# Zero rows below the operands of a few tensor products

## The chip, the cores and the metric

One NeuronCore of a Trainium2 chip runs the whole program in one launch. The metric is the device time in microseconds (us) of an execution. The kernel before takes 1612.25 us, the median of three runs (1609.80 to 1613.06 us).

TensorE (PE) multiplies, ScalarE (ACT) and VectorE (DVE) do the element-wise work and read the matmul results, GpSimd (POOL) prepares constants and a few small steps, SyncE (SP) issues most DMAs. Each engine works through its own list in order and waits at semaphores for the others.

## The reference

The input x has 32 batches of 128 tokens with 128 features, and a context of the same shape. Four layers follow, each an attention on the context and then a feed-forward part; each part adds `tanh(gate) * part(layernorm(x))` to x. What matters here are the biases and one selection:

```python
# layer 0, attention: the output product has a bias bo
out = out @ Wo + bo
# layer 0, feed-forward: a short convolution along the tokens with a bias conv_b per feature
# layer 1, feed-forward: 3-tap convolution over 512 hidden features, with bias
h = depthwise_conv1d(h.transpose(0, 2, 1), conv_w, conv_b)
# layer 2, attention
pv = jnp.einsum('nle,fe->nlf', v, Wv) + bv
# layer 2, feed-forward: one of 8 experts for each token, by the argmax of a softmax
probs = jax.nn.softmax(x @ Wg + bg, axis=-1)
e_idx = jnp.argmax(probs, axis=-1) % 8
h = jax.nn.relu(jnp.einsum('bsd,edf->besf', x, We) + be[None, :, None, :])
out = jnp.einsum('besf,bse->bsf', h, onehot) * p[..., None]
```

## The kernel before, in words

The program runs eight stages one after the other: A0, F0, A1, F1, A2, F2, A3, F3 (A is attention, F is feed-forward, the digit is the layer). Each stage goes over eight chunks of four batches (CB = 4, 512 tokens). x stays in SBUF. A stage starts a chunk when the stage before has finished that chunk of x (semaphore `x_done`). Inside a stage the order of each engine's instructions is written out by hand in Python functions, with a loop over pairs of chunks; PE issues the first products of chunk c + 1 between the last ones of chunk c.

A matmul takes a stationary operand (loaded by a LDWEIGHTS instruction, which the profile lists as the engine PEld) and a moving operand; both lie on partitions, and the number of partitions is the number of rows that are summed over. An f32 product is two passes, so two LDWEIGHTS and two MATMUL records.

A bias is added by a product of its own that opens the accumulation in PSUM: a stationary operand of ones times the bias. In before.py these products have few rows:

- L936, stage A0, one per chunk: `ones[0:1, :]` times one row of `bo0`, f32, 1 row, ahead of the output products L938.
- L1102, stage F0, `conv`, one per chunk: `ones[0:1, :]` times `cb0`, f32, 1 row, ahead of the 16 convolution products L1105.
- L1269, stage F1, `up(c, p, j)`, four per chunk: `ones3` times `cbias1`, bf16, 3 rows. The three rows are the three bf16 parts into which the f32 bias is split (`parts`), so that the sum is exact. The three f32 tap products L1271 follow. Around them `integers_T` (L1279, transposes of the quantised hidden values) and `down` (L1288) of three steps earlier are issued. `down` waits for ACT's copy of those transposes (L1460) and, at the first step of a chunk, for DVE's update of x (L2408).
- L1168, stage A2, `projected`, one per chunk: `ones3` times `biasv2`, bf16, 3 rows, ahead of the value products L1170.
- L1325, stage F2, `logits`, one per chunk: `ones3` times `bias2`, bf16, 3 rows, ahead of L1327.
- L1339, stage F2, `spread(c, e)`, eight per chunk: `select2[:, e, :]` times `ohT2[0:E2, :]`, bf16, 8 rows. It copies row e of the transposed one-hot choice onto all 128 partitions; DVE multiplies the tokens by it (L2490, `masked`), and the expert product L1347 uses the masked tokens. `spread` runs four experts ahead.
- L1343, stage F2, `bias`, one per chunk: `bepart2[0]` times `ohT2`, bf16, 24 rows (8 experts, three parts each).

In F2 `chosen` (L1334) transposes the one-hot choice `oh2` that DVE makes at L2483, ACT copies it to `ohT2` (L1821), and the first `spread` of the next chunk waits for that copy. DVE's order in a chunk is: masked 0 to 3, residual, masked 4, masked 5, the argmax with L2474 to L2483, masked 6 and 7, normalisation.

POOL prepares the constants: those of A1, A2, F1 and F0 after its last share of A0, those of F2 after its last share of F1; after each it waits for DVE's variance (`power`, L602).

Of the kernel before, what the change touches and what calls it, by code (L numbers as in the profile page):

```python
# [6 lines left out]
BF16 = mybir.dt.bfloat16  # L7
# [53 lines left out]
RING2 = 4  # L61
# [76 lines left out]
def flamingo(nc, a, out):  # L138
    ctx = ExitStack()
    with ctx:  # L140
        def sb(name, shape, dt=F32):
            return ctx.enter_context(nc.sbuf_tensor(name, shape, dt))
# [26 lines left out]
        ident16 = sb("ident16", [P, P], BF16)  # L169
        ones = sb("ones", [P, P])  # L170
# [32 lines left out]
        def ar(shape, dt=F32):  # L203
            n = 1
            for s in shape[1:]:
                n *= s
            words = n if dt != BF16 else (n + 1) // 2
            v = arena[0:shape[0], used[0]:used[0] + words]
            used[0] += words
            assert used[0] <= ARENA  # L210
            v = v if dt == F32 else v.bitcast(dt)
            if len(shape) == 3:
                v = v.rearrange("p (a b) -> p a b", a=shape[1])
            if len(shape) == 4:
                v = v.rearrange("p (a b c) -> p a b c", a=shape[1], b=shape[2])
            return v
# [5 lines left out]
        lastdi3 = sb("last_places", [P, SC], U32)  # L222
        wq0, wkv0 = sb("wq0", [P, P]), sb("wkv0", [P, 2, 4 * D0])
        wkvs0 = sb("wkvs0", [P, KV0])
        wo0, bo0 = sb("wo0", [P, P]), sb("bo0", [P, P])
        bq0row, bq0 = sb("bq0row", [P, P]), sb("bq0", [P, CB * HEADS, D0])
        bk0g, bv0g, bkv0 = sb("bk0g", [P, 4 * D0]), sb("bv0g", [P, 4 * D0]), sb("bkv0", [P, KV0])
        wr0, rb0 = sb("wr0", [P, R0]), sb("rb0", [P, R0])
        wg0, wu0 = sb("wg0", [P, E0 * I0]), sb("wu0", [P, E0 * I0])
        wd0 = sb("wd0", [P, 2, P])  # L230
        cw0, cb0 = sb("cw0", [P, TAPS0]), sb("cb0", [1, P])
        wT1 = sb("wT1", [P, 3, P])
        causal = sb("causal", [P, P])
        w1q, w2q = sb("w1q", [P, H1], BF16), sb("w2q", [P, K1, P], BF16)
# [35 lines left out]
        wconv1 = ar([P, 3, H1])  # L270
        cb1, cbrest1 = ar([3, H1]), ar([3, H1])
        cbpart1 = [ar([3, H1], BF16) for _ in range(3)]
        cbias1, ones3 = ar([3, H1], BF16), ar([3, P], BF16)
        be2, berest2, bemask2 = ar([3 * E2, P]), ar([3 * E2, P]), ar([3 * E2, 3])
        bepart2 = [ar([3 * E2, P], BF16) for _ in range(3)]
        bg2, bgrest2 = ar([3, P]), ar([3, P])
        bgpart2 = [ar([3, P], BF16) for _ in range(3)]
        bias2 = ar([3, CB, P], BF16)
        select2 = ar([E2, E2, P], BF16)
        causal16 = ar([P, CB, P], BF16)  # L280
        bv2, bvrest2 = ar([3, P]), ar([3, P])
        bvpart2 = [ar([3, P], BF16) for _ in range(3)]
        biasv2 = ar([3, CB, P], BF16)

        fresh()
        wide0 = ar([P, CB, E0, I0])
# [31 lines left out]
        top2, nmx2, idx2, idf2 = ar([P, CB, 8]), ar([P, CB]), ar([P, CB, 8], U32), ar([P, CB])  # L318
        ex2, ps2, pg2 = ar([P, CB, P]), ar([P, CB]), ar([P, 2, CB])
        oh2 = ar([P, CB, 3 * E2])  # L320
        ohT2 = ar([3 * E2, W], BF16)
        xnT2 = [xnT, ar([P, W])]
        xm2 = ar([P, RING2, W])
        yT2 = ar([P, W])
# [85 lines left out]
        def context(p):  # L410
# [7 lines left out]
        ]  # L418
        SETUP_LOADS = [
            (graw[:, 0:4], rows(a["g_xattn"])), (graw[:, 4:8], rows(a["g_ffn"])), (graw[:, 8:9], rows(a["L3_xattn_gate"])),  # L420
            (bo0[:, :], rows(a["L0_xattn_bo"])),
            (wr0[:, :], a["L0_ffn_Wr"]), (rb0[:, :], rows(a["L0_ffn_router_bias"])),
            (wg0[:, :].rearrange("p (e i) -> p e i", e=E0), a["L0_ffn_Wg"].rearrange("e h i -> h e i")),
            (wu0[:, :].rearrange("p (e i) -> p e i", e=E0), a["L0_ffn_Wu"].rearrange("e h i -> h e i")),
# [12 lines left out]
            (wo3[:, :, :], a["L3_xattn_w_out"].rearrange("(k p) d -> p k d", p=P)), (bo3[:, :], rows(a["L3_xattn_b_out"])),  # L437
            (keyT[:, 0, :], a["L3_ffn_keys"]), (keyT[:, 1, :], a["L3_ffn_rw"]), (rb3[:, :], rows(a["L3_ffn_rb"])),
            (b13[:, :, :], a["L3_ffn_b1"].rearrange("e (k p) -> p e k", p=P)),
        ]  # L440

        WD = []
# [5 lines left out]
        s_const = sem("constants_ready")  # L448
# [31 lines left out]
        def _(sp):  # L480
            with nc.allow_non_contiguous_dma(reason="small vectors laid along the partitions"):
                sp.dma_start(FIRST_LOADS[0][0], FIRST_LOADS[0][1]).then_inc(s_first, 16)
                sp.dma_start(context(0), cview[:, 0:CB, :]).then_inc(s_cx[0], 16)
                for dst, src in FIRST_LOADS[1:]:
                    sp.dma_start(dst, src).then_inc(s_first, 16)
                sp.dma_start(context(1), cview[:, CB:2 * CB, :]).then_inc(s_cx[1], 16)
                sp.dma_start(wo0[:, :], a["L0_xattn_Wo"]).then_inc(sem("wo0_loaded"), 16)
                sp.dma_start(x[:, 2 * CB:B, :], a["x"][2 * CB:B].rearrange("b t d -> t b d")).then_inc(sem("x_loaded"), 16)
                for dst, src in SETUP_LOADS:
                    sp.dma_start(dst, src).then_inc(s_load, 16)  # L490
            for dst, src in WD:
                sp.dma_start(dst, src).then_inc(s_wd, 16)

# [80 lines left out]
        def _(pl):  # L574
# [85 lines left out]
            def thrice(of):  # L660
                return of[:, :].unsqueeze(1).to_broadcast([3, CB, P])
# [1 line left out]
            pl.wait_ge(s_load, 16 * n_loads)  # L663
            pl.tensor_copy(causal16[:, :, :], causal[:, :].unsqueeze(1).to_broadcast([P, CB, P])).then_inc(sem("A12_constants"), 1)
            parts(bv2, bvrest2, bvpart2, lambda i: ident[0:3, i:i + 1])
            pl.tensor_tensor(biasv2[:, :, :], thrice(bvpart2[0]), thrice(bvpart2[2]), ALU.add).then_inc(sem("A12_constants"), 1)
            rest = cb1
            for i in range(3):
                step(pl.tensor_copy(cbpart1[i][:, :], rest[:, :]))
# [2 lines left out]
                rest = cbrest1  # L672
            for i in range(3):
                step(pl.tensor_scalar(cbpart1[i][:, :], cbpart1[i][:, :], ident[0:3, i:i + 1], None, ALU.mult))
            step(pl.tensor_tensor(cbias1[:, :], cbpart1[0][:, :], cbpart1[1][:, :], ALU.add))
            pl.tensor_tensor(cbias1[:, :], cbias1[:, :], cbpart1[2][:, :], ALU.add).then_inc(sem("F1_constants"), 1)
            pl.memset(ones3[:, :], 1.0).then_inc(sem("F1_constants"), 1)
            pl.wait_ge(s_setup, WEIGHTS)
            for t in range(3):
# [38 lines left out]
            step(pl.affine_select(out=bemask2[:, :], in_=bemask2[:, :], compare_op=ALU.is_ge, fill=0.0, base=E2 - 1,  # L718
                                  pattern=[[E2, 3]], channel_multiplier=-1))
            parts(be2, berest2, bepart2, lambda i: bemask2[:, i:i + 1])  # L720
            pl.tensor_tensor(bepart2[0][:, :], bepart2[0][:, :], bepart2[2][:, :], ALU.add).then_inc(sem("F2_constants"), 1)
            parts(bg2, bgrest2, bgpart2, lambda i: ident[0:3, i:i + 1])
            pl.tensor_tensor(bias2[:, :, :], thrice(bgpart2[0]), thrice(bgpart2[2]), ALU.add).then_inc(sem("F2_constants"), 1)
            pl.tensor_copy(select2[:, :, :], ident16[0:E2, 0:E2].unsqueeze(2).to_broadcast([E2, E2, P])).then_inc(sem("F2_constants"), 1)
            with pl.Fori(0, NC) as c:
                power("A2", c)
            with pl.Fori(0, NC) as c:
# [77 lines left out]
        def _(pe):  # L805
# [41 lines left out]
            def heads0():  # L847
# [35 lines left out]
                def body(c, p, more, first=False, live=True):  # L883


                    for w in range(STEPS0 if live else DRAIN0):
# [43 lines left out]
                        if tile:  # L930
                            cc, _, j = tile
                            if j == 0:
                                if first:
                                    pe.wait_ge(s_load, 16 * n_loads)
                                pe.wait_ge(s_xdone, cc + 1)
                                nc.tensor.matmul(bank[7][:, :], ones[0:1, :], bo0[0:1, :].unsqueeze(1).to_broadcast([1, CB, P]), start=True, stop=False)  # L936
                            pe.wait_ge(sem("A0_oT"), cc * CB + (j + 3))
                            nc.tensor.matmul(bank[7][:, j * P:j * P + P], oT0[:, j % 2, :], wo0[:, :], start=False, stop=(j == CB - 1))\  # L938
                                .then_inc(sem("A0_y"), 1)
# [158 lines left out]
            def conv(c):  # L1098

                pe.wait_ge(sem("F0_conv_in"), c + 1)  # L1100
                pe.wait_ge(s_xdone, c + (NC * STAGE["F0"] + 1))
                nc.tensor.matmul(bank[5][:, :], ones[0:1, :], cb0[:, :].unsqueeze(1).to_broadcast([1, CB, P]), start=True, stop=False)  # L1102
                for j in range(CB):
                    for k in range(TAPS0):
                        nc.tensor.matmul(bank[5][:, j * P:j * P + P], cin0[:, j, k:k + P], taps0[:, k, :], start=False, stop=False)  # L1105
# [230 lines left out]

            def spread(c, e):
                pe.wait_ge(sem("F2_masked"), c * E2 + (e + 1))
                nc.tensor.matmul(bank[2 + e % RING2][:, :], select2[:, e, :], ohT2[0:E2, :], start=True, stop=True).then_inc(sem("F2_spread"), 1)  # L1339

            def bias(c):
                pe.wait_ge(sem("F2_relu"), c + 1)
                nc.tensor.matmul(bank[6][:, :], bepart2[0][:, :], ohT2[:, :], start=True, stop=False).then_inc(sem("F2_bias"), 1)  # L1343

            def expert(c, e):
                pe.wait_ge(sem("F2_masked"), c * E2 + (e + 1 + RING2))
# [112 lines left out]
        def _(act):  # L1459
# [1201 lines left out]
```

## Time and profile before

| what | value |
|---|---|
| median of three runs | 1612.25 us (1609.80 to 1613.06) |
| profiled execution, its own time | 1613.21 us |
| its span, first to last instruction | 1611.4 us |
| PE busy | 1416.8 us, 88% |
| PE weight loads | 1027.8 us, 64% |
| DVE busy | 1106.9 us, 69% |
| ACT busy | 1023.7 us, 64% |
| POOL busy | 543.4 us, 34% |
| share of PE in the chain that ended last | 68% |
| mean granted TensorE clock | 0.957 |

Busy time is a union of the instructions' durations; since matmuls are pipelined, the duration of one (for example 0.38 us) is longer than the distance from its start to the next one's start (for example 0.22 us). The distance between starts is what a stream of matmuls costs. A clock of 1.00 is the upper of TensorE's two levels (2.4 GHz), 0.50 the lower (1.2 GHz).

### The profile page before, as it was taken

How to read it: one execution, taken by the hardware profiler on the slowest of the kernel's cores; microseconds unless marked ns; L12 is line 12 of the kernel's file. 1: busy time of each engine (PE TensorE's matmuls, PEld its weight loads, DVE VectorE, ACT ScalarE, POOL GpSimd, SP SyncE). 2: the span in 40 equal slices, each digit the busy share in tenths (PEclk: the TensorE clock that was granted, in tenths of full speed). 3: DMA queues.
4: the chain of work that ended last, by engine and by line, in shares of the span. 5: the costliest groups of instructions: out<-in, count | busy, mean ns of one | idle time of the engine just before them, and what ended most of it. 6: DMA issues, size and time to landing. Idle time of an engine off the chain costs nothing.

```text
span 1611.4 us, 35134 instructions
## 1 busy us (share of the span) xinstructions
PE 1416.8 (88%) x9978; PEld 1027.8 (64%) x9982; DVE 1106.9 (69%) x3551; ACT 1023.7 (64%) x2947; POOL 543.4 (34%) x627
## 2 busy tenths in 40 slices
PE   2788888998989989899999989999997389999994
PEld 2566655666734446343466666666666289999994
DVE  1788887688767656787467767777777546666665
ACT  2688887554545556222778868788875367777762
POOL 5354466222211221001001413422433635555550
PEclk9899999999989999899999999999997589999998
DMA  8000049700299931000000100100032322222227
GB/s 193 24 8 7 13 69 164 103 0 7 60 165 164 166 49 38 1 1 0 8 8 2 35 19 18 35 22 13 28 125 89 103 60 66 63 67 66 67 58 261
DMA packets 143559, 98.41 MB, mean 61 GB/s; under 512 B 20610, under 2 KB 132652, under 8 KB 142292
## 3 DMA queue, kind: packets, MB, share of 16 engines
q1 hardware_dynamic: 134740, 80.15, 26.1%
q0 software_dynamic: 8704, 16.87, 3.2%
q8 instruction: 55, 0.90, 0.2%
q14 instruction: 60, 0.49, 0.1%
HBM read 43.10 MB, written 54.93 MB: 61 GB/s over the span
## 4 chain that ended last, share of the span: by engine, by line
PE 68%; ACT 11%; DVE 10%; issue 7%; POOL 2%; DMA 1%; SPq 0%; DVEq 0%; ACTq 0%; POOLq 0%
PE bank L983 7%; PE bank L1427 7%; PE bank L1419 7%; PE bank L1271 5%; PE bank L999 4%; PE bank L1034 4%; PE bank L1347 4%; PE bank L924 4%; ACT arena L1460 3%; PE bank L1019 3%; ACT att L1597 3%; PE bank L987 3%; PE bank L1009 3%; ACT att L1462 2%; PE bank L906 2%
## 5 line engine op out<-in xcount | busy, mean ns | idle before, releaser
L1460 ACT ACTIVATE arena<-bank 128x512 f32<-128x512 f32 (+7 forms) x396 | 254.9, 672 | 155.6 <-PE bank L1334 57.9
L1881 ACT ACTIVATE att<-bank,arena 128x128 f32<-128x128 f32 x576 | 165.0, 371 | 73.2 <-PE bank L1419 73.0
L800 POOL DMA_INDIRECT expert_outputs<-arena x144 | 143.6, 997 | 146.6 <-DVE arena L2601 133.2
L1597 ACT ACTIVATE att<-bank,arena 128x128 f32<-128x128 f32 x512 | 180.7, 396 | 15.7 <-DVE arena L2119 14.7
L754 POOL DMA_INDIRECT dispatched_rows<-arena x112 | 115.4, 1030 | 172.0 <-DVE arena L2027 84.6
L602 POOL TENSOR_TENSOR ve<-mv,eps 128x4 f32<-128x4 f32 x64 | 12.9, 202 | 462.8 <-DVE mv L1943 454.9
L1427 PE MATMUL bank<-arena,att 128*128 128x128 f32 x1152 | 153.9, 277 | 1.0 <-ACT att L1881 0.3
L1419 PE MATMUL bank<-xnT,arena 128*128 128x128 f32 x1152 | 154.0, 277 | 0.2 <-ACT xnT L1460 0.2
L1427 PEld LDWEIGHTS bank<-arena,att 128*128 128x128 f32 x1152 | 140.9, 193 | 3.1 <-ACT att L1881 3.1
L1419 PEld LDWEIGHTS bank<-xnT,arena 128*128 128x128 f32 x1152 | 141.6, 194 | 0.6 <-ACT xnT L1460 0.6
L1597 ACT ACTIVATION_READ_ACCUMULATOR att<-bank,arena 128x1 f32 x512 | 120.9, 236 | 0.0
L2587 DVE COPY arena<-arena 128x512 f32 x144 | 61.6, 427 | 83.0 <-issue 82.9
L1460 ACT ACTIVATE xnT<-bank 128x128 f32<-128x128 f32 (+1 forms) x180 | 63.6, 354 | 85.3 <-PE bank L821 35.6
L2119 DVE TENSOR_REDUCE arena<-bank 128x4 f32<-128x512 f32 x128 | 82.4, 685 | 49.6 <-PE bank L999 49.4
L1582 ACT ACTIVATE arena<-bank 128x512 f32<-128x512 f32 x128 | 76.1, 615 | 58.1 <-PE bank L983 58.1
L2042 DVE TENSOR_REDUCE nmx<-bank 128x8 f32<-128x1024 f32 x64 | 78.0, 1219 | 44.4 <-PE bank L895 43.9
L924 PE MATMUL bank<-ident,att 128*128 128x128 f32 x512 | 69.6, 279 | 28.7 <-ACT att L1462 28.3
L1271 PE MATMUL bank<-arena 128*128 128x512 f32 x192 | 92.5, 618 | 0.0
L2125 DVE TENSOR_TENSOR att<-att,arena 128x512 f32<-128x512 f32 x128 | 89.2, 696 | 4.9 <-DVE arena L2124 0.5
L999 PE MATMUL bank<-arena 64*128 64x128 f32 x1024 | 78.2, 293 | 13.2 <-ACTq L1589 6.6
L999 PEld LDWEIGHTS bank<-arena 64*128 64x128 f32 x1024 | 65.5, 195 | 34.5 <-issue 27.1
L924 PEld LDWEIGHTS bank<-ident,att 128*128 128x128 f32 x512 | 55.9, 142 | 45.6 <-ACT att L1462 45.3
(360 smaller groups left out, 3255.1 us busy)
## 6 DMA issues: line engine op xcount, KB each, us to landing
dispatched_rows<-padf SPq DMA_DIRECT2D x16, 2128.5 KB, 34.7
arena<-dispatched_rows SPq DMA_DIRECT2D x144, 64.5 KB
cxT<-in_ctx SPq DMA_DIRECT2D x32, 256.0 KB, 2.8
arena<-in_L_ffn_w SPq DMA_DIRECT2D x8, 1024.0 KB
arena<-expert_outputs SPq DMA_DIRECT2D x8, 1024.0 KB, 13.9
expert_outputs<-arena POOLq DMA_INDIRECT x144
out_x<-x SPq DMA_DIRECT2D x8, 256.0 KB, 4.3
dispatched_rows<-arena POOLq DMA_INDIRECT x112
```

Source lines behind the costliest of these rows:

```text
L754: pl.indirect_dma_start(sent, bass.IndirectOffsetOnAxis(places[:, q:q + 1], 0), held[:, q, :], None)\
L800: pl.indirect_dma_start(sent_out, bass.IndirectOffsetOnAxis(xtu3[:, s, P:P + 1], 0), yt3[:, s, :], None, bounds_check=TOP3 * TOKENS - 1, o ...
L924: last = nc.tensor.transpose(bank[2 + k][:, i * P:i * P + P], ex[:, v % 2 * 2 + k, i, :], ident[:, :])
L983: last = nc.tensor.matmul(A[:, :], wqk3[:, t, pair * P:pair * P + P], cxT[:, p, :] if t else xnT[:, :], start=True, stop=True)
L999: last = nc.tensor.matmul(bank[side][:, i * P:i * P + P], q, k, start=True, stop=True)
L1271: last = nc.tensor.matmul(bank[1 + j][:, :], xsT1[:, p * CB + j, t:t + P], wconv1[:, t, :], start=False, stop=(t == 2))
L1419: last = nc.tensor.matmul(bank[s % 2][:, k * P:k * P + P], w1c3[:, s % 4, k * P:k * P + P], xnT[:, (s % 4) * P:(s % 4) * P + P], start=Tru ...
L1427: last = nc.tensor.matmul(bank[2 + s % 2][:, 0:P], h3[:, s % 2, k * P:k * P + P], w2c3[:, s % 4, k * P:k * P + P], start=(k == 0), stop=(k ...
L1460: copy = lambda o, i: nc.scalar.activation(o, i, ACT.Copy)
L1597: last = nc.scalar.activation(ex3_of(w, side)[:, i, :], bank[side][:, i * P:i * P + P], ACT.Exp, bias=nm3[:, w % 2, h:h + 1], accum_out=su ...
L1881: last = nc.scalar.activation(h3[:, s % 2, k * P:k * P + P], bank[s % 2][:, k * P:k * P + P], ACT.Gelu, bias=b1c3[:, s % 4, k:k + 1])
L2125: v.tensor_tensor(ex3_of(w, side), ex3_of(w, side), rs3[:, w % 2, side:2 * HQ:2].unsqueeze(2).to_broadcast([P, HQ, P]), ALU.mult) .then_in ...
```

## The change

The few-row operands become operands of 128 rows, in which all rows behind the old ones are zero (in `ones` and `ones3` they are ones, against zero rows of the other operand). Names: `bo0` becomes `boz0`, loaded as one row into a zeroed tile by the last setup load, which waits for POOL's constants; `cb0` is copied into the zeroed `cbz0`; `cbias1`, `ones3`, `bias2`, `biasv2`, `select2` and `ohT2` get 128 partitions; `be16` is new and takes the sum of `bepart2`. `ohT2` moves to the arena's part for constants, where it is zeroed once; ACT's copy still writes its first 24 rows. POOL gets nine memsets and one copy. Number, order and columns of all matmuls stay as they are.

```diff
-        cbias1, ones3 = ar([3, H1], BF16), ar([3, P], BF16)
+        cbias1, ones3 = ar([P, H1], BF16), ar([P, P], BF16)
-        bias2 = ar([3, CB, P], BF16)
-        select2 = ar([E2, E2, P], BF16)
+        bias2 = ar([P, CB, P], BF16)
+        select2 = ar([P, E2, P], BF16)
+        be16 = ar([P, P], BF16)
+        ohT2 = ar([P, W], BF16)
-        biasv2 = ar([3, CB, P], BF16)
+        biasv2 = ar([P, CB, P], BF16)
...
-            (bo0[:, :], rows(a["L0_xattn_bo"])),
+            (boz0[0:1, :], a["L0_xattn_bo"].rearrange("(a d) -> a d", a=1)),
...
-                for dst, src in SETUP_LOADS:
+                for dst, src in SETUP_LOADS[:-1]:
                     sp.dma_start(dst, src).then_inc(s_load, 16)
+                sp.wait_ge(s_const, 1)
+                sp.dma_start(SETUP_LOADS[-1][0], SETUP_LOADS[-1][1]).then_inc(s_load, 16)
...
+            pl.memset(boz0[:, :], 0.0)
...
+            step(pl.memset(biasv2[:, :, :], 0.0))
+            pl.tensor_tensor(biasv2[0:3, :, :], thrice(bvpart2[0]), thrice(bvpart2[2]), ALU.add).then_inc(sem("A12_constants"), 1)
+            step(pl.memset(cbias1[:, :], 0.0))
+            pl.memset(ohT2[:, :], 0.0)
...
+            step(pl.memset(cbz0[:, :], 0.0))
+            pl.tensor_copy(cbz0[0:1, :], cb0[:, :])
...
+            step(pl.memset(be16[:, :], 0.0))
+            step(pl.memset(bias2[:, :, :], 0.0))
+            step(pl.memset(select2[:, :, :], 0.0))
...
-                                nc.tensor.matmul(bank[7][:, :], ones[0:1, :], bo0[0:1, :].unsqueeze(1).to_broadcast([1, CB, P]), start=True, stop=False)
+                                nc.tensor.matmul(bank[7][:, :], ones[:, :], boz0[:, :].unsqueeze(1).to_broadcast([P, CB, P]), start=True, stop=False)
...
-                nc.tensor.matmul(bank[5][:, :], ones[0:1, :], cb0[:, :].unsqueeze(1).to_broadcast([1, CB, P]), start=True, stop=False)
+                nc.tensor.matmul(bank[5][:, :], ones[:, :], cbz0[:, :].unsqueeze(1).to_broadcast([P, CB, P]), start=True, stop=False)
...
-                nc.tensor.matmul(bank[2 + e % RING2][:, :], select2[:, e, :], ohT2[0:E2, :], start=True, stop=True).then_inc(sem("F2_spread"), 1)
+                nc.tensor.matmul(bank[2 + e % RING2][:, :], select2[:, e, :], ohT2[:, :], start=True, stop=True).then_inc(sem("F2_spread"), 1)
...
-                nc.tensor.matmul(bank[6][:, :], bepart2[0][:, :], ohT2[:, :], start=True, stop=False).then_inc(sem("F2_bias"), 1)
+                nc.tensor.matmul(bank[6][:, :], be16[:, :], ohT2[:, :], start=True, stop=False).then_inc(sem("F2_bias"), 1)
```

## Rows read from the trace of the kernel before

**Rows 1.** Busy time by stretch: length, busy of each engine, clock, DMA share, GB/s.

```profile
451.00:579.00 128.00, 120.19 (x490) 56.18 (x490) 87.48 (x342) 70.68 (x129) 28.41 (x48) 0.98 1.19 156
641.00:756.00 115.00, 109.76 (x372) 46.20 (x371) 92.45 (x349) 25.17 (x88) 10.87 (x18) 0.93 0.00 1
```

**Rows 2.** Few-row products by line: count, ns min/median/max, first and last start us, shape.

```profile
L1269 PE MATMUL bank<-arena x32: 382/385/604, 453.2 to 575.0; 3*128 3x512 bf16 x32
L1339 PE MATMUL bank<-arena x64: 374/384/629, 651.8 to 751.8; 8*128 8x512 bf16 x64
```

**Rows 3.** Timeline of PE in F2: start us, us from first start to last end.

```profile
671.78 0.38 PE L1339 MATMUL bank<-arena 8*128 8x512 bf16 x1
672.00 0.38 PE L1325 MATMUL bank<-arena 3*128 3x512 bf16 x1
672.31 1.16 PE L1327 MATMUL bank<-wg,xnT 128*128 128x128 f32 x8
...
675.95 1.98 PE L1347 MATMUL bank<-arena,we 128*128 128x512 f32 x4
677.77 0.60 PE L1334 MATMUL bank<-ident,arena 128*24 128x128 f32 x4
678.21 1.88 PE L1347 MATMUL bank<-arena,we 128*128 128x512 f32 x4
680.02 0.39 PE L1339 MATMUL bank<-arena 8*128 8x512 bf16 x1
```

**Rows 4.** The same timeline in A1, around a 128-row bf16 product.

```profile
430.67 0.39 PE L1186 MATMUL bank<-arena,ident 128*128 128x512 bf16 x1
430.89 1.05 PE L1190 MATMUL bank<-arena 128*128 128x128 f32 x8
```

**Rows 5.** Timeline of all engines in F1; in brackets idle before, and releaser.

```profile
507.13 0.58 ACT L1460 ACTIVATE arena<-bank 128x512 bf16<-128x512 bf16 x1
507.77 0.40 PE L1288 MATMUL bank<-w2q,arena 128*128 128x128 bf16 x4
508.32 0.38 PE L1269 MATMUL bank<-arena 3*128 3x512 bf16 x1
508.63 0.30 PEld L1271 LDWEIGHTS bank<-arena 128*128 128x128 f32 x2 [0.23 <-issue]
508.63 2.84 PE L1271 MATMUL bank<-arena 128*128 128x512 f32 x6
511.51 0.60 ACT L1790 ACTIVATE arena<-bank 128x512 f32<-128x512 f32 x1 [1.79 <-PE bank L1271]
...
516.37 0.34 PE L1288 MATMUL bank<-w2q,arena 128*128 128x128 bf16 x3 [0.92 <-DVE x L2408]
```

**Rows 6.** Timeline of DVE: the one-hot choice in F2.

```profile
676.76 0.26 DVE L2483 TENSOR_TENSOR arena<-iota,arena 128x96 f32<-128x96 f32 x1
```

**Rows 7.** Timeline of DVE in A2.

```profile
622.69 1.13 DVE L2334 SCALAR_TENSOR_TENSOR x<-bank,rsg,x 128x128 f32 x4 [0.31 <-PE bank L1208]
```

**Rows 8.** Timeline in A0, behind the bias product.

```profile
133.51 1.12 PE L936 MATMUL bank<-bo,ones 1*128 1x512 f32 x2
134.57 0.49 PE L938 MATMUL bank<-wo,arena 128*128 128x128 f32 x2
134.93 1.05 ACT L1462 ACTIVATE att<-att 128x1024 f32<-128x1024 f32 x1
136.11 1.09 PE L924 MATMUL bank<-ident,att 128*128 128x128 f32 x8
```

**Rows 9.** Who waited for whom in F0: us in total, times, longest us.

```profile
PE bank L1113 <- ACT arena L1460: 5.8, 7, 1.1
```

**Rows 10.** Timeline of POOL: a memset, and its first wait behind the constants of F2.

```profile
4.03 0.54 POOL L609 MEMSET arena<- 64x512 bf16 x1
574.39 0.28 POOL L602 TENSOR_TENSOR ve<-mv,eps 128x4 f32<-128x4 f32 x1 [5.16 <-DVE mv L1943]
```

**Rows 11.** Busy time in a stretch of A3, columns as in rows 1.

```profile
954.00:963.00 9.00, 6.94 (x47) 6.44 (x47) 1.29 (x2) 3.69 (x17) 3.83 (x4) 0.62 0.14 42
```

More of the change, by code:

```diff
@@ L224, in flamingo @@
         wkvs0 = sb("wkvs0", [P, KV0])
-        wo0, bo0 = sb("wo0", [P, P]), sb("bo0", [P, P])
+        wo0 = sb("wo0", [P, P])
         bq0row, bq0 = sb("bq0row", [P, P]), sb("bq0", [P, CB * HEADS, D0])
@@ L231, in flamingo @@
         cw0, cb0 = sb("cw0", [P, TAPS0]), sb("cb0", [1, P])
+        cbz0 = sb("cbz0", [P, P])
+        boz0 = sb("boz0", [P, P])
         wT1 = sb("wT1", [P, 3, P])
@@ L320, in flamingo @@
         oh2 = ar([P, CB, 3 * E2])
-        ohT2 = ar([3 * E2, W], BF16)
         xnT2 = [xnT, ar([P, W])]
@@ L665, in _ @@
             parts(bv2, bvrest2, bvpart2, lambda i: ident[0:3, i:i + 1])
-            pl.tensor_tensor(biasv2[:, :, :], thrice(bvpart2[0]), thrice(bvpart2[2]), ALU.add).then_inc(sem("A12_constants"), 1)
+            step(pl.memset(biasv2[:, :, :], 0.0))
+            pl.tensor_tensor(biasv2[0:3, :, :], thrice(bvpart2[0]), thrice(bvpart2[2]), ALU.add).then_inc(sem("A12_constants"), 1)
+            step(pl.memset(cbias1[:, :], 0.0))
+            pl.memset(ohT2[:, :], 0.0)
             rest = cb1
@@ L674, in _ @@
                 step(pl.tensor_scalar(cbpart1[i][:, :], cbpart1[i][:, :], ident[0:3, i:i + 1], None, ALU.mult))
-            step(pl.tensor_tensor(cbias1[:, :], cbpart1[0][:, :], cbpart1[1][:, :], ALU.add))
-            pl.tensor_tensor(cbias1[:, :], cbias1[:, :], cbpart1[2][:, :], ALU.add).then_inc(sem("F1_constants"), 1)
+            step(pl.tensor_tensor(cbias1[0:3, :], cbpart1[0][:, :], cbpart1[1][:, :], ALU.add))
+            pl.tensor_tensor(cbias1[0:3, :], cbias1[0:3, :], cbpart1[2][:, :], ALU.add).then_inc(sem("F1_constants"), 1)
             pl.memset(ones3[:, :], 1.0).then_inc(sem("F1_constants"), 1)
@@ L720, in _ @@
             parts(be2, berest2, bepart2, lambda i: bemask2[:, i:i + 1])
-            pl.tensor_tensor(bepart2[0][:, :], bepart2[0][:, :], bepart2[2][:, :], ALU.add).then_inc(sem("F2_constants"), 1)
+            step(pl.memset(be16[:, :], 0.0))
+            step(pl.memset(bias2[:, :, :], 0.0))
+            step(pl.memset(select2[:, :, :], 0.0))
+            pl.tensor_tensor(be16[0:3 * E2, :], bepart2[0][:, :], bepart2[2][:, :], ALU.add).then_inc(sem("F2_constants"), 1)
             parts(bg2, bgrest2, bgpart2, lambda i: ident[0:3, i:i + 1])
-            pl.tensor_tensor(bias2[:, :, :], thrice(bgpart2[0]), thrice(bgpart2[2]), ALU.add).then_inc(sem("F2_constants"), 1)
-            pl.tensor_copy(select2[:, :, :], ident16[0:E2, 0:E2].unsqueeze(2).to_broadcast([E2, E2, P])).then_inc(sem("F2_constants"), 1)
+            pl.tensor_tensor(bias2[0:3, :, :], thrice(bgpart2[0]), thrice(bgpart2[2]), ALU.add).then_inc(sem("F2_constants"), 1)
+            pl.tensor_copy(select2[0:E2, :, :], ident16[0:E2, 0:E2].unsqueeze(2).to_broadcast([E2, E2, P])).then_inc(sem("F2_constants"), 1)
             with pl.Fori(0, NC) as c:
@@ L1820, in chosen_T @@
                     act.wait_ge(sem("F2_bias"), c)
-                copy(ohT2[:, :], bank[0][0:3 * E2, :]).then_inc(sem("F2_ohT"), 1)
+                copy(ohT2[0:3 * E2, :], bank[0][0:3 * E2, :]).then_inc(sem("F2_ohT"), 1)
             def exponentials(c):
```

## Prediction

> **What bounds the kernel now.** Begin with the page: the chain that ended last is PE for 68% of the span. A change to PE's stream can therefore count, if it lies in stages that PE bounds. The busy time by stretch says which: in F1 PE is busy 120.2 of 128 us, in F2 109.8 of 115, both near the full clock (0.98 and 0.93) [rows 1]. The lines with few rows come next: L1269 has 32 records in F1, L1339 has 64 in F2 [rows 2]; by the loops, L1168, L1325 and L1343 have 8 each, and L936 and L1102 have 8 products of two passes each. The durations in that view say nothing, since matmuls overlap. The timeline of PE does, read by distances between starts.
>
> Take F2 [rows 3]. From L1334 at 677.77 to L1347 at 678.21 four transposes cost 0.44, 0.11 each. A 512-column f32 pass, of which L1347 has four between 678.21 and 680.02, costs 1.81/4; in the clean stretches elsewhere it is 0.43, so 1.72 for the four, and 0.09 is left over, just ahead of the 8-row L1339. The four passes that follow an L1339 (675.95 to 677.77) take 1.82: 0.10 too much, this time just behind it. And the L1339 at 671.78 costs 0.22 when the 3-row L1325 follows at 672.00, but that one costs 0.31 when the 128-row L1327 follows. So a few-row product is itself no slower than its 512 columns (0.22). What costs is each change between few rows and 128 rows: about 0.10 going in, 0.10 coming out, and 0.10 more behind the first 128-row pass (half of that behind a bf16 or identity transpose). The weight loads show why: the two LDWEIGHTS of L1271 begin only at 508.63, together with its first matmul, after 0.23 of idle [rows 5]; they weren't loaded ahead. The counter-example is in A1: L1186 is bf16, 512 columns, 128 rows, and the f32 product behind it starts 0.22 later, at 430.89 [rows 4]. No stall on a product that is the same but for its rows.
>
> **The change, part by part.** It leaves every product in its place with 128 rows in both operands, so the changes of rows go.
>
> *Price of one.* An isolated one, such as L1269, saves 0.10 + 0.10 + 0.10 = 0.30 on PE (508.32 to 508.63 is 0.31 where rows 4 have 0.22, and so on) [rows 4, 5]. A group of four L1339 ahead of transposes saves 0.10 + 0.09 + 0.05 = 0.24, once. The 1-row f32 product L936 takes 133.51 to 134.57, 1.06 where two passes are 0.86; with 0.09 ahead and 0.10 behind that is 0.39 [rows 8].
>
> The Trainium skill weighs in on both sides. "TensorEngine Tiling (Array Packing)", Key Properties, has it that changing the tiling mode drains TensorE, which would be this stall, and the trace agrees. "TensorE: Matmul & The Clock Gate", in the table "Why this matters for your kernels", says that a single matmul with K = 32 takes the same time as one with K = 128; by that alone widening would give nothing, which is rival A.
>
> *F2.* One chunk of PE holds a group of four (0.24), L1343 (0.30), L1339 ahead of a transpose (0.25), L1339 with L1325 (0.30) and two isolated L1339 ahead of L1347 (0.30 each): 1.68 of the 12.93 between 667.09 and 680.02. But PE isn't alone there. L1334 transposes what DVE makes at L2483, which ends at 677.02, and L1334 starts at 677.77 [rows 3, 6]: 0.75 later. All the savings of the chunk lie ahead of L1334, while DVE's order up to L2483 is one unbroken run that starts with the first L1339; after 0.75 PE waits for it. The same pair stands 1.13, 0.75, 0.56, 0.35, 0.56, 0.56 and 1.13 apart in the seven chunks that have it, 5.03 in sum. To each, 0.09 is added (no stall ahead of the next chunk's L1339, behind L1334) and a wake-up of 0.05 taken off: 5.3. The last chunk has no such pair but three masked products of DVE at its end: 0.25. The L1325 before the first chunk: 0.25. F2 gives 5.8, of at most 8 x 1.68 = 13.4.
>
> *F1.* Four L1269 a chunk, 0.30 each. Two are covered. Behind the second one, PE's L1288 waits for ACT's copy (507.13 + 0.58 = 507.71, L1288 at 507.77) [rows 5]; ACT is busy without a break from the silu of the first one, so that one gains nothing. The last of a chunk runs beside the DVE run that begins with the silu of the third (ACT L1790 at 511.51) and ends with x, for which PE has idled 0.92 before 516.37; its gain becomes idle time. Two count: 0.60 in each of five middle chunks, 3.0. The first chunk has no ACT wait behind the second product, but a half-clock start: 1.0. In the seventh DVE does less and three count, 0.9. In the last all four, less the one behind a wait: 1.1. F1 gives 6.0, of at most 32 x 0.30 = 9.5.
>
> *A2.* PE runs back to back; the period could fall by 0.30. The next in line is DVE's loop, which idles 0.31 for PE at L2334 [rows 7]: just enough. One of eight products lies in the end of F1, where PE waits anyway; six at 0.28 and the half-clock one at 0.3 give 2.0, of at most 2.4.
>
> *A0.* 0.39 a chunk on PE, and the products behind L936 would come earlier, but L924 at 136.11 waits for ACT's exponential, which ends at 134.93 + 1.05 = 135.98 [rows 8]. In all eight chunks the next L924 hangs on ACT or on the setup. I take 0, the other end is 8 x 0.39 = 3.1.
>
> *F0.* Behind L1102 and L1105, PE waits for ACT before L1113 in seven chunks, 5.8 in all [rows 9], 0.8 each. So 0.39 counts in the first chunk alone: 0.4, at most 3.1.
>
> *POOL.* A 512-element bf16 memset over 64 partitions took 0.54 [rows 10]; nine memsets and a copy are an estimated 5 us. The tightest place is ahead of 574.39, where POOL waits 5.16 behind the constants of F2 [rows 10]: 128 + 512 + 1024 elements, 1.8 by that row. Even at twice that it is hidden. The memsets of A1, F1 and F0 have 8.6 of waiting behind them, boz0 comes while the first loads are in flight. Without cover F2's would cost 1.8.
>
> *SP.* The last setup load now waits for POOL's constants, done at about 4 us, while SP issues it at about 33; the weight loads behind it on the queue don't wait either. A 64 KB broadcast becomes 0.5 KB. Nothing.
>
> Sum: 5.8 + 6.0 + 2.0 + 0 + 0.4 = 14.2 us. The profiled execution took 1613.2 (span 1611.4 and 1.8 around it), so 1599.0 for it; against the median of 1612.25, **1598 us**.
>
> **The rivals.**
>
> A. *Row count is not the cause.* The stall could come from the arena's few-row source tiles, or from the wait ahead of the product; then the 128-row ones stall as well and the time is 1612. For it: most few-row products stand behind a semaphore wait. Against: L1186 has such a wait in front too and doesn't stall, and L1325 behind L1339 is free [rows 3, 4].
>
> B. *More reaches the end than I let through.* If the waits for ACT and DVE move up with PE (because I took for an unbroken run what itself hangs on PE), the sum goes to PE's full 1.68 in F2 and 0.30 in F1: 13.4 + 9.5 + 2.4 + 0.4 = 25.7 us, and 1586.5. For it: PE idles so little in both [rows 1]. Against: the gaps of 0.75 and of 0.92 [rows 3, 5, 6].
>
> C. *The clock of A3 turns it slower.* The stretch 954 to 963 in A3 ran at a mean of 0.62: PE had idled there (6.94 busy in 9) [rows 11]. A mean of 0.62 over 9 us is 3.4 us of full-rate time lost, 6.8 us spent at the lower level, so a fall costs up to 3.4. All of A3 now begins 14 us earlier against whatever the clock goes by; if the falls came in five more of its chunks than before, 5 x 3.4 = 17 us would outweigh the 14.2, and 1615 would stand. It decides from five falls on. Against: PE idles no longer than before there, and only two chunks of A3's main part fall now. One fall more or less is quite possible and is in my range.
>
> **How the numbers follow.** My forecast has 0.73, A 0.07, B 0.15, C 0.05. A change under 0.2% (3.2 us) can't be told from none here. Faster by more: forecast and B, 0.88; within: A, 0.07; slower: C, 0.05. The range: the cover of each term is read to about 30% (4 us), a clock fall is 3.4 us either way, and the three runs shown spread 3 us. That gives 1592 to 1605 for the forecast alone; to leave no more than 2 in 10 out it reaches some way to B: 1589 to 1605.
>
> **What would show it.** Right: L1271's weight loads start ahead of its first matmul; L1269 costs 0.22 to the next start; the period in F2 falls from 12.93 to about 12.2 with L1334 now waiting for DVE's L2483; in F1 PE's wait for L2408 grows from 0.92 to 1.2 and a chunk shortens by 0.6; A0 and F0 keep their lengths but for 0.4; A3 and F3 keep theirs. Wrong: a stall in front of a 128-row L1339 (A), or an F2 period near 11.3 (B), or an unchanged start of A3. A wait of POOL under 1 us before A2's first variance would show the memsets dearer than taken.

## The result, and the profile after

The changed kernel took 1593.8 us (median of 6 runs, 1591.0 to 1595.8) beside 1611.0 for the kernel before (6 runs, 1608.5 to 1613.1): a ratio of 0.9895 [0.9881, 0.9909]. The same kernel once more (e10 below, on chip 15) gave 0.9896 [0.9879, 0.9912]. That is 17 us, where 14.2 were forecast; of the 4 us below the forecast of 1598, 1.2 are the kernel before itself, whose six runs have a median 1.2 lower than its first three. The chain of waits has less PE in it (61% for 68%) and more of DVE (13% for 10%) and ACT (13% for 11%). From the page of after (span, busy times, with POOL's eight memsets and one copy more, 636 instructions for 627, and the chain by engine):

```profile
span 1593.0 us, 35147 instructions
PE 1386.4 (87%) x9982; PEld 1032.8 (65%) x9982; DVE 1106.8 (69%) x3551; ACT 1023.0 (64%) x2947; POOL 547.8 (34%) x636
PE 61%; ACT 13%; DVE 13%; issue 8%; POOL 2%; DMA 1%; DVEq 1%; SPq 0%; ACTq 0%; POOLq 0%
```

Every line of PE is 14 further down now: L1339 is L1353 (the spread), L1343 is L1357, L1325 is L1339, L1334 is L1348 (`chosen`), L1347 is L1361 (the expert's passes), L1269 and L1271 are L1283 and L1285, L1288 is L1302, L924 is L938; DVE's L2483 is L2497, L2490 is L2504; ACT's L1460 and L1462 are L1474 and L1476.

PE's timeline in F2, after. It answers to [rows 3]:

```profile
672.57 0.38 PE L1353 MATMUL bank<-arena 128*128 128x512 bf16 x1
672.78 1.88 PE L1361 MATMUL bank<-arena,we 128*128 128x512 f32 x4
675.48 0.61 PE L1348 MATMUL bank<-ident,arena 128*24 128x128 f32 x4 [0.82 <-DVE arena L2497]
676.15 1.98 PE L1361 MATMUL bank<-arena,we 128*128 128x512 f32 x4
677.97 1.03 PE L1353 MATMUL bank<-arena 128*128 128x512 bf16 x4
...
684.16 0.38 PE L1353 MATMUL bank<-arena 128*128 128x512 bf16 x1
684.38 1.02 PE L1361 MATMUL bank<-arena,we 128*128 128x512 f32 x2
```

L1353 costs 0.21 or 0.22 to the next start (672.57 to 672.78, 684.16 to 684.38), whatever stands on either side. And L1348 now waits 0.82 for DVE's one-hot, where before it came 0.75 behind it.

The timeline of F1, after, answers to [rows 5]. The weight loads of L1285 begin at 497.46, 0.22 ahead of its first pass and beside the bias product. L1302's wait for x is 1.29, from 0.99 for the same chunk of before (the next chunk, the one shown in [rows 5], went from 0.92 to 1.22):

```profile
496.54 0.40 PE L1302 MATMUL bank<-w2q,arena 128*128 128x128 bf16 x4 [1.29 <-DVE x L2422]
...
497.46 0.38 PE L1283 MATMUL bank<-arena 128*128 128x512 bf16 x1
497.46 0.41 PEld L1285 LDWEIGHTS bank<-arena 128*128 128x128 f32 x2
...
497.68 1.02 PE L1285 MATMUL bank<-arena 128*128 128x512 f32 x2
```

A0 shows a stall that goes and is given back at once, PE's timeline against [rows 8]. L950 costs 0.86 (131.88 to 132.74) where L936 cost 1.06. The next L938 (L924 in before, where it had no idle time ahead of it, 136.11 in [rows 8]) waits 0.46 for ACT's exponential:

```profile
131.88 1.02 PE L950 MATMUL bank<-boz,ones 128*128 128x512 f32 x2
132.74 0.39 PE L952 MATMUL bank<-wo,arena 128*128 128x128 f32 x2
...
134.57 1.09 PE L938 MATMUL bank<-ident,att 128*128 128x128 f32 x8 [0.46 <-ACT att L1476]
```

Where the time went, by the starts of the same instructions on PE in four profiles. Each row is the time from the mark of the row above to its own mark (us; e1 is the changed kernel with the old rows and e10 the changed kernel once more, both below):

| up to | before | e1 | after | e10 | forecast saving |
|---|---|---|---|---|---|
| F0's first convolution, from the start | 295.75 | 295.57 | 293.79 | 293.54 | 0 |
| A1's first scores | 107.45 | 107.41 | 107.37 | 107.36 | 0.4 |
| A1's last scores | 37.78 | 37.78 | 37.80 | 37.80 | 0 |
| A2's last scores (F1, A2) | 193.27 | 193.35 | 184.93 | 185.22 | 6.0 + 2.0 |
| first `chosen` of F2 | 15.80 | 15.81 | 14.89 | 15.98 | 0.25 |
| second `chosen` | 14.79 | 14.81 | 11.85 | 12.47 | 1.2 |
| last `back` | 92.83 | 92.84 | 89.82 | 89.87 | 4.4 |
| first product of F3's tiles (A3) | 536.42 | 533.39 | 534.83 | 532.71 | 0 |
| end of span (F3) | 317.34 | 317.01 | 317.70 | 317.19 | 0 |

F1 and A2 gave what was forecast. F2's total is near it, but made up otherwise: 2.3 to 2.9 in its first chunk and 3.0 in the other seven. Some 2 us come from the stretch before F0, where nothing was forecast. The row of A3 differs by 3.0 us between before and e1, which have the same products throughout, and tells nothing by itself.

### The profile page after: what moved, and what is told of

Read it like the earlier page. It is cut to its first block, busy times and chain, and to the rows that moved or that the text cites. A ratio compares the mean times of both kernels' runs of the same rounds, so it can differ in the third digit from the quotient of the medians.

```text
span 1593.0 us, 35147 instructions
## 1 busy us (share of the span) xinstructions
PE 1386.4 (87%) x9982; PEld 1032.8 (65%) x9982; DVE 1106.8 (69%) x3551; ACT 1023.0 (64%) x2947; POOL 547.8 (34%) x636
## 4 chain that ended last, share of the span: by engine, by line
PE 61%; ACT 13%; DVE 13%; issue 8%; POOL 2%; DMA 1%; DVEq 1%; SPq 0%; ACTq 0%; POOLq 0%
PE bank L997 7%; PE bank L1441 7%; PE bank L1433 7%; PE bank L1013 4%; ACT arena L1474 4%; PE bank L1048 4%; PE bank L1285 3%; PE bank L938 3%; PE bank L1033 3%; ACT att L1611 3%; PE bank L1001 3%; PE bank L1023 3%; ACT att L1476 2%; PE bank L920 2%; PE bank L1361 2%
## 5 line engine op out<-in xcount | busy, mean ns | idle before, releaser
L1474 ACT ACTIVATE arena<-bank 128x512 f32<-128x512 f32 (+7 forms) x396 | 255.0, 672 | 149.6 <-PE bank L1348 54.5
L1474 ACT ACTIVATE xnT<-bank 128x128 f32<-128x128 f32 (+1 forms) x180 | 63.6, 353 | 80.1 <-PE bank L835 34.3
L938 PE MATMUL bank<-ident,att 128*128 128x128 f32 x512 | 70.0, 280 | 32.2 <-ACT att L1476 32.0
L1285 PE MATMUL bank<-arena 128*128 128x512 f32 x192 | 89.7, 604 | 0.0
L938 PEld LDWEIGHTS bank<-ident,att 128*128 128x128 f32 x512 | 56.3, 142 | 49.1 <-ACT att L1476 48.4
```

The costliest lines, as they stand in the source:

```text
L938: last = nc.tensor.transpose(bank[2 + k][:, i * P:i * P + P], ex[:, v % 2 * 2 + k, i, :], ident[:, :])
L1285: last = nc.tensor.matmul(bank[1 + j][:, :], xsT1[:, p * CB + j, t:t + P], wconv1[:, t, :], start=False, stop=(t == 2))
L1474: copy = lambda o, i: nc.scalar.activation(o, i, ACT.Copy)
```

## The experiments

**How many rows does it take?** Four kernels have all of the change's set-up (memsets, copy, moved load) and another number of rows in the seven products; e1 has the old ones (1, 3, 8, 24). The edit is shown for `spread`, the other six read the same number of rows:

```
-    matmul(bank[2 + e % RING2], select2[:, e, :], ohT2[:, :])
+e1  matmul(bank[2 + e % RING2], select2[0:8, e, :], ohT2[0:8, :])
+e2  matmul(bank[2 + e % RING2], select2[0:32, e, :], ohT2[0:32, :])
+e3  matmul(bank[2 + e % RING2], select2[0:64, e, :], ohT2[0:64, :])
+e4  matmul(bank[2 + e % RING2], select2[0:65, e, :], ohT2[0:65, :])
```

> All of the change's set-up (memsets, copy, moved load) stays, but the seven products read only their old 1, 3, 8 or 24 rows again. Theory (the gain is all in the products' rows): the time of the kernel before, ratio 1.000 within 0.002, and L1285 again 0.31 behind its bias product. Rival (moving the load and zeroing matter): 2 to 4 us below the kernel before.

> The seven products read 32 rows of the widened tiles. Theory (a change of TensorE's row tiling stalls, and 32 rows are the same tiling as 3 or 8): no gain, ratio 1.000 within 0.002. Rival (few active rows as such make it slow, or the old tiles in the arena do): a part of the gain, above 4 us, or all of it, 17.

> The same with 64 rows. Theory (row tiling): 64 rows are still another tiling than 128, so the stalls of 0.10 stay on both sides and the ratio is 1.000 within 0.002. Rival (cost falls with the rows): about half of the 17 us.

> The same with 65 rows, one more than e3. Theory (row tiling, more than 64 rows take the whole array): the full gain, ratio 0.9895 within 0.002, no stall at the bias products. Rival (only exactly 128 rows match the neighbours): no gain, 1.000.

Measured: e1 1.0002 [0.9992, 1.0012], e2 1.0003 [0.999, 1.0015], e3 0.9993 [0.998, 1.0006], e4 0.99 [0.9883, 0.9918]. The set-up costs nothing that can be measured. Everything hangs on the 65th row. PE's timeline in F2, first of e3, then of e4:

```profile
673.90 0.39 PE L1353 MATMUL bank<-arena 64*128 64x512 bf16 x1
674.21 1.12 PE L1361 MATMUL bank<-arena,we 128*128 128x512 f32 x2
675.27 0.39 PE L1353 MATMUL bank<-arena 64*128 64x512 bf16 x1
675.59 1.98 PE L1361 MATMUL bank<-arena,we 128*128 128x512 f32 x4
```

```profile
672.89 0.38 PE L1353 MATMUL bank<-arena 65*128 65x512 bf16 x1
673.11 1.02 PE L1361 MATMUL bank<-arena,we 128*128 128x512 f32 x2
673.97 0.38 PE L1353 MATMUL bank<-arena 65*128 65x512 bf16 x1
674.19 1.88 PE L1361 MATMUL bank<-arena,we 128*128 128x512 f32 x4
```

The same source, semaphores and neighbours; from one spread to the next it is 1.37 at 64 rows (673.90 to 675.27) and 1.08 at 65. The same pair stands 1.37 apart at 8 rows (before and e1) and at 32 (e2), and 1.08 at 128. So the stall is neither the arena's nor the wait's (rival A), and it isn't graded: 1.37 less 1.08 is the 0.30 of the prediction within 0.01. What TensorE does in the stall, no run shows. It has the shape of the drain on a change of tiling mode in the Trainium skill's "TensorEngine Tiling (Array Packing)", Key Properties; that page gives no time for it.

**Do the stages add up?** e5 has 128 rows in F2's products alone, e6 in all but F2's.

```
 e5  # A0, F0, A2, F1: rows as before; F2: 128
 e6  # A0, F0, A2, F1: 128; F2: select2[0:8], be16[0:24], bias2[0:3]
```

> Only F2's three products (L1339, L1343, L1325) read 128 rows, the other four read their old rows. Theory (stalls plus a cover by DVE, and in F2's first chunk a clock that rises earlier): 5.5 to 7 us below the kernel before, ratio 0.996. Rival (F2 yields PE's full 1.68 a chunk once A2 no longer feeds it late): 13 us, 0.992. Rival (terms of the stages aren't additive, all of the gain needs all stages): under 3 us.

> The reverse: A0, F0, F1 and A2 at 128 rows, F2 at the old rows. Theory (additive): F0 0.4, F1 5.2, A2 about 2 to 3, so 8 to 9 us below before, ratio 0.9948, and together with e5 the 15 to 17 us of the whole. Rival (not additive): the sum of both is off by more than 4 us.

Measured: e5 1621.11, 0.9958 [0.994, 0.9976]; e6 1621.10, 0.9956 [0.9941, 0.9971]; before 1628.03 on that chip. 6.9 us each, 13.9 together; the intervals (3 us either way) hold both this and the 17 of the whole. F2 and the rest have a share of about one half each (5.8 and 8.4 were forecast); e6 is 1 to 2 us short of what was expected of it, within its interval.

**Why did F2's first chunk give 2.3 to 2.9 us?** It runs at the lower level of the clock (0.50 in the rows) at first. In the changed kernel the clock rises sooner. e7 is the changed kernel with the first four spreads of that chunk (RING2 is 4) at 8 rows, e8 the old rows with these four at 128; e12 and e11 do the same with every product of that chunk, and with the logits' bias of chunks 0 and 1:

```
 e7   rows = 8 if c == 0 and e < RING2 else 128      # the spread alone
 e8   rows = 128 if c == 0 and e < RING2 else 8
 e12  rows = 8 (24, 3) if c == 0 else 128        # spread, bias, logits' bias
 e11  rows = 128 if c == 0 else 8 (24, 3)
```

> The changed kernel, with only the first four spread products of F2's chunk 0 at 8 rows. Theory C (few-row products hold the granted clock at its lower level longer): the clock rises 6.5 us behind the first spread instead of 3.0 to 4.2, and chunk 0 (first to second L1348) takes about 14 us instead of 11.9 to 12.4. Theory S (only stalls): the rise stays at 3.0 to 4.2, chunk 0 takes at most 0.3 more. In total 2 us or 0.3 us, both near the noise; the profile decides.

> Old rows everywhere, with only the first four spread products of F2's chunk 0 at 128 rows. Theory C: the clock rises 3 to 4 us behind the first spread instead of 6.5 to 7.1, and chunk 0 takes about 13 us instead of 14.8. Theory S: 14.5 to 14.8 and the rise stays late. Total within 0.2% of before in both.

> The set-up of the changed kernel and the old row counts everywhere but in the first chunk of F2, which has all its products at 128 rows (8 spreads, one output bias, the logits' bias of chunks 0 and 1). Theory S (stalls alone, at whatever clock stands): five or six changes of rows go, most of them at half clock, and the clock rises when it rises, 6.2 to 7.4 us behind the first spread as in the runs with few-row products there: the chunk takes 14.0 to 14.4 us from `chosen` to `chosen`, not 14.8. Theory C (in this chunk the few-row products also hold the clock down): the rise comes 3 to 4.2 us behind the first spread, as in all five profiles with the wide products, and the chunk takes 11.9 to 12.5. In time S says about 0.6 us below before, C about 2.7 (0.9983).

> The inverse: the changed kernel with the old row counts in all products of F2's first chunk. S: the rise at 3 to 4.2 us stays, the chunk takes 12.5 to 13. C: the rise comes at 6.2 to 7.4 us and the chunk takes 14.8 to 15.2; the time is about 2.7 us above the changed kernel's, a ratio of 0.9912 to before where that one had 0.9895.

Measured: e7 0.9916 [0.9883, 0.995], e8 1.0003 [0.9991, 1.0015], e11 0.9966 [0.9951, 0.9982], e12 0.9911 [0.9894, 0.9929]. Two stretches of 3 us from the chunk's first spread on (length; busy time of PE, PEld, DVE, ACT, POOL; granted clock; DMA share, GB/s), of before, after, e11 and e12:

```profile
651.76:654.76 3.00, 3.00 (x6) 1.06 (x7) 2.21 (x4) 1.32 (x8) 0.00 (x0) 0.50 0.02 5
654.76:657.76 3.00, 3.00 (x8) 1.32 (x7) 1.21 (x4) 0.06 (x1) 0.00 (x0) 0.50 0.00 0
```

```profile
640.49:643.49 3.00, 3.00 (x7) 1.29 (x8) 2.21 (x4) 1.32 (x8) 0.00 (x0) 0.50 0.00 0
643.49:646.49 3.00, 3.00 (x17) 1.87 (x16) 2.15 (x8) 0.60 (x1) 0.00 (x0) 0.99 0.00 0
```

```profile
650.09:653.09 3.00, 3.00 (x7) 1.29 (x8) 2.21 (x4) 1.31 (x8) 0.00 (x0) 0.50 0.00 0
653.09:656.09 3.00, 3.00 (x14) 1.51 (x13) 1.84 (x7) 0.60 (x1) 0.00 (x0) 0.87 0.00 0
```

```profile
641.64:644.64 3.00, 3.00 (x6) 1.06 (x7) 2.21 (x4) 1.32 (x8) 0.00 (x0) 0.50 0.00 0
644.64:647.64 3.00, 3.00 (x8) 1.31 (x7) 1.21 (x4) 0.06 (x1) 0.00 (x0) 0.50 0.00 0
```

In the second stretch the clock is back (0.99, 0.87) where the chunk has no few-row product and still 0.50 where it has. In all 14 profiles:

| first chunk of F2 | clock rises, us behind the first spread | `chosen` to `chosen` |
|---|---|---|
| all at 128 (65) rows: after, e4, e5, e9, e10, e11 | 3.1, 4.2, 3.1, 3.8, 3.9, 3.8 | 11.85, 12.41, 11.87, 12.42, 12.47, 12.23 |
| few rows: before, e1, e2, e3, e6, e12 | 6.6, 6.6, 6.7, 7.1, 7.4, 7.4 | 14.79, 14.81, 14.83, 15.06, 15.19, 15.21 |
| mixed: e7, e8 | 6.3, 6.2 | 13.51, 14.85 |

Six of six against none of eight, and by e11 and e12 it goes with this chunk's own products, not with what comes before or behind. Nor does it go with how long before the first spread the clock fell: in e11 it fell 3.0 us ahead of it and stayed at 0.50 for 6.8 us, in e12 2.8 ahead and stayed for 10.2. All six kernels of the first line have 6.8 there, all eight others 10.2 or, where it didn't rise in between, 17.1. In e11 and e12 theory C of their expectations stands and S falls: the stalls of that chunk alone would save an estimated 0.4 to 0.8 us by the expectation of e11, and the chunk gives 2.3 to 3.4. e8 went against its theory C, which wanted the rise at 3 to 4 and a chunk of 13: four wide spreads don't bring the rise forward. Four few-row ones are enough to undo the early rise (e7, 6.3). What in the stalls holds the clock down the rows don't tell: PE is shown as busy for 3.00 of 3.00 in all. The run times agree where they can: e12 lies 3.5 us above e10 (by medians, on the same chip at another time, where the kernel before had moved by 1.2; the ratios' intervals overlap). e11 gained 5.3 us, more than the 2.6 of its chunk; A3's beginning had no clock fall in e11's profile, while before has one of 6.8 us at 784.6, which may be the rest. Falls there lasted 6.8 us in seven of the eight profiles with few-row products in F2's first chunk (3.4 in e7), and 3.4, 3.4, 3.4, 0, 0, 0 in the other six. A fall of 6.8 us at half clock costs up to 3.4. That this goes with the change, too, is likely by the count, and was not tested by itself.

**Is DVE what is left in F2?** The changed kernel makes PE wait for DVE ahead of `chosen`. e9 starts DVE's run sooner: the next chunk's spreads 0 and 1 go ahead of expert 7.

```
+    if e == 6 and more:
+        pe.wait_ge(sem("F2_ohT"), c + 2)
+        spread(c + 1, 0)
+        spread(c + 1, 1)
```

Its lines of DVE are five further down again: L2497 is L2502 there, L2504 is L2509.

> The changed kernel with PE's order in F2 turned: the spreads of experts 0 and 1 of the next chunk are issued behind expert 6 and ahead of expert 7, not at the head of their chunk. The DVE run that ends in the one-hot of the second choice begins with the masked copies of these two, so it can begin about 1.7 us earlier (expert 7's four passes). Theory D (what is left in F2 is PE waiting for DVE, at `chosen` and again at expert 6): both waits go, the period falls from 12.25 to 12.9 to about 12.2, PE's first expert-6 pass follows `chosen` by 0.44 instead of 0.67, and the time is 2 to 4 us below the changed kernel's. Theory P (PE's own stream is the period, the stalls gone being all there was): the period and the time stay within 0.5 us of the changed kernel's. If DVE's own work of a chunk is the limit (about 12 us of it), the period stops there and the gain is nearer 2 than 4.

> The changed kernel itself, on the same chip as e9, so that the two can be set side by side: 0.989 of the kernel before by all theories. By the clock rows of the other profiles the first rise of the clock in F2 comes 3 to 4.2 us behind the first spread, against 6.5 to 7.4 with few-row products in its first chunk; if it comes at 6 or more here, that difference was chance.

Measured, on one chip: e9 1590.46 us, 0.9876 [0.9856, 0.9895]; e10 1593.18, 0.9896 [0.9879, 0.9912]. By the medians e9 is 2.7 us faster; the intervals overlap. In the profiles it is plain: from the first `chosen` to the last `back` 99.72 in e9 and 102.34 in e10, and periods of 11.9 to 12.4. P falls. DVE's waits in F2 between 664 and 726, of before, after and e9 (in total, times, longest), show DVE's idle time for PE being used up (664 to 726 holds about five periods of each, not the same ones):

```profile
DVE arena L2490 <- PE bank L1339: 6.2, 5, 1.7
```

```profile
DVE arena L2504 <- PE bank L1353: 4.1, 5, 0.8
```

```profile
DVE arena L2509 <- PE bank L1353: 0.2, 1, 0.2
```

So D's last clause holds: DVE's own work is the period now. In these 62 us of e9 it waits 1.1 in all for anything but its own instructions, and it is busy for 11.3 to 11.6 of three periods of 12.0 to 12.4. One thing that I expected there failed. The 0.67 from `chosen` to expert 6 stayed, PE and DVE in e9:

```profile
677.05 0.26 DVE L2502 TENSOR_TENSOR arena<-iota,arena 128x96 f32<-128x96 f32 x1
677.29 1.29 DVE L2509 TENSOR_TENSOR arena<-bank,xnT 128x512 f32<-128x512 f32 x2
677.37 0.61 PE L1348 MATMUL bank<-ident,arena 128*24 128x128 f32 x4
...
678.04 1.12 PE L1361 MATMUL bank<-arena,we 128*128 128x512 f32 x2
```

DVE writes the masked operand of expert 6 right behind the one-hot (L2509, 0.69 for the first), whenever that comes. e9 is the fastest of all kernels tried, by its median.

## Why the prediction was right, step by step

**The price of one** was right: 0.22 from the widened product to its neighbour, nothing ahead of it and nothing behind; 0.30 for one between f32 passes, in F2 (e3 and e4), in F1, and six times 0.30 in A2.

**F1 and A2** were right in their sum, 8.0 forecast and 8.05 to 8.34 measured, and in F1's five middle chunks, which fell by 0.58 each: of the four products L1283 in a chunk, the first and the third bring 0.30, the second and the fourth nothing (the starts of L1285 behind them, at the middle chunk's four: -3.84, -4.14, -4.14, -4.44 against before). The sum hides two errors that cancel. F1 alone gave 5.1 and not 6.0 (DVE's lead over before grows from 2.0 to 7.1; 5.6 from e1 to e10): its first chunk 0.6 and not 1.0 (1.1 from e1 to e10), its last two 1.4 and not 2.0. A2 gave 3.2 (2.5 from e1 to e10) and not 2.0: six times 0.30 as forecast, and more at its beginning, which runs at half clock and was put at 0.3.

**A0 and F0** were right on the cover. In A0 from the second projection on to the last, e10's lead over e1 stays between 1.63 and 2.03: each L950 brings 0.39, and the next wait for ACT takes it back. F0 gave 0.4: L1102's own savings are 0.28 ahead of the first convolution and 0.39 behind it, of which 0.30 are lost again ahead of A1's first scores. But the lead of 1.6 itself is not in the sum. It is complete by 83 us (0.40 at the first projection, 66.2, 1.63 at the second). F0 began at 294.7 to 295.8 in the seven profiles with 64 rows or fewer in A0, and at 293.5 to 295.2 in the seven with 65 or 128, 1.3 less in the mean.

Most of that is the clock, and it doesn't go with the rows. In e1 the clock falls once more at 78.0, for 3.4 us; in e10 it doesn't. But e4, with 65 rows in A0, has that fall, and e11, with the old row there, hasn't. The stretch from 77 to 83 of e1, e10, e4 and e11, in this order (the number behind POOL's count is the clock):

```profile
77.00:83.00 6.00, 4.92 (x29) 2.73 (x30) 4.70 (x9) 2.25 (x3) 1.49 (x6) 0.72 0.15 44
```

```profile
77.00:83.00 6.00, 4.34 (x35) 2.98 (x35) 5.36 (x10) 3.62 (x5) 2.75 (x8) 1.00 0.15 44
```

```profile
77.00:83.00 6.00, 5.04 (x29) 3.42 (x30) 4.59 (x9) 2.25 (x3) 2.15 (x8) 0.72 0.15 44
```

```profile
77.00:83.00 6.00, 5.28 (x44) 3.78 (x43) 5.23 (x10) 3.62 (x7) 1.95 (x7) 1.00 0.15 44
```

From ACT's L1476 near 78 to its next L1474 of 1024 columns (83.27 in e1) it is 5.21 us in e1 and 5.32 in e4, 3.71 in e10 and 3.72 in e11: the fall costs 1.5. At 200 us the lead over e1 is 1.63 in e10 and e12, but 0.01 in e4 and -0.02 in e6, all with 65 or 128 rows in A0, and 0.83 in e11 with the old row. The lead of after itself, 1.39, is there by 68 us: its falls at 39 and 70 lasted 3.4 us, where that of e10 at 38 and that of e1 at 68 lasted 6.8. What the products themselves give ahead of F0's first convolution is 0.11 at the end of A0 and the 0.28 of L1102. One thing stays open: the first rise came at 34.5 to 36.0 us in six of the seven profiles with 65 or 128 rows in A0, and at 43.6 to 46.8 in the other eight profiles, though no product that differs has run by then. e4, e6, e10 and e12 gain 0.8 by it, and the fall at 38 takes 0.7 of that back.

**F2** was right in its total by two errors that cancel, 5.8 forecast with 0.25 of it ahead of the first `chosen`, 5.3 to 5.9 measured from there to the last `back`.

- The step "after 0.75 PE waits for it" missed a second wait. I took expert 6 to follow the four transposes of `chosen` by 0.44, as in [rows 3]. But its masked operand is the next thing that DVE makes behind the one-hot. As long as `chosen` came late, that was done; now all is on DVE's heels:

```profile
675.17 0.26 DVE L2497 TENSOR_TENSOR arena<-iota,arena 128x96 f32<-128x96 f32 x1
675.41 1.29 DVE L2504 TENSOR_TENSOR arena<-bank,xnT 128x512 f32<-128x512 f32 x2
```

  From L1348 to L1361 it is 0.67 (675.48 to 676.15), not 0.44, and the four passes behind it take 1.82 again: 0.33 a chunk. The six periods behind the first chunk fell by 0.68, 0.34, 0.05, 0.32, 0.27 and 1.26 where 0.79, 0.60, 0.39, 0.60, 0.60 and 1.17 were forecast, 2.9 for 4.2. They are 11.7 to 12.9 long, not about 12.2, at which the forecast put them in its list of signs.
- The first chunk was costed by its stalls and a lead, 1.17. It gave 2.3 to 2.9, since the clock's rise moved too. I had the clock in a rival, but only as a danger in A3, and not as something that the stalls themselves delay.

**Rivals.** A is dead by e3 and e4. B (25.7 us, or 25.8 with the 32 x 0.30 = 9.6 of F1 that the prediction has as 9.5) is off: `chosen` waits for DVE as in the forecast, and F2's period is nowhere near 11.3 but in its last full one (11.7). C, more clock falls in A3, didn't come: A3 has two in its main part in before (784.6 and 955.3) and two in after (769.8 and 937.1), and the table's last two rows, A3 and F3, are 0.7 shorter and 0.2 longer in e10 than in e1. POOL's estimated 5 us were 4.4 (543.4 to 547.8) for eight memsets and a copy, not nine memsets; they are hidden, as e1 shows.

The time came out 4 us under the forecast, within its range: 1.2 by the runs of before, and the rest, as far as the profiles tell, by the lead in A0, which is mostly a clock fall more or less, and by A3's beginning, neither of which is in the sum. The price of a stall and the cover in A0, F0 and the middle of F1 were understood. That F1 and A2 together, and F2 as a whole, came out within 0.5 us of their terms was in part luck, since errors of 0.4 to 1.8 us cancelled in each.

## What to carry to other kernels

Look for matmuls whose contraction has 64 rows or fewer among ones of 128: the sign is a start-to-start distance of 0.31 where the product has 0.22 of work, and the next weight load beginning only with its own matmul. Zero rows up to 128 (65 are enough) take it away, and the wider product costs PE no more than the few-row one (0.22 from its start to the next). Before adding up the gain, follow what the neighbour waits for on the slower engine: here not only its result, but also the next one that it makes. And where such products stand in a stretch at the lower clock, their removal can bring the rise forward, which here was worth more than the stalls of that chunk. Before a lead is credited to a change, see whether the clock fell the same number of times: one fall of 3.4 us made 1.5 us of lead in A0, with either number of rows.

## What the runs showed of the hardware that was not expected

- The stall doesn't depend on the number of rows up to 64: one spread to the next is 1.37 us at 8, 32 and 64 rows, 1.08 at 65 and 128; the whole kernel is 0.9993 at 64 and 0.99 at 65.
- With few-row products in F2's first chunk the clock came back 6.2 to 7.4 us behind the first spread (8 profiles), without them 3.1 to 4.2 (6 profiles), at the same busy time of PE. 128 rows in that chunk's products alone brought the rise to 3.8 (e11), few rows in them alone to 7.4 (e12); four spreads of the chunk at 128 rows did not bring it forward (6.2, e8).
